# Attention value products on the quarters of the output partitions instead of the halves

## The chip, the cores and the metric

The kernel runs on one core of one Trainium2 chip. The metric is the device time of an execution in microseconds (us); lower is better. Three executions of the kernel before took 770.21, 770.67 and 775.93 us, so its time is given as the median, 770.67 us.

## What is computed

Four residual blocks follow one another on an image of 4 x 32 x 32 pixels with 32 channels, each on the channel-normalized input: a deformable convolution, a neighbourhood attention, a state-space block with three scan directions, and a convolution with learned offsets. Only the attention is touched. Cut to what matters:

```
qkv = x @ w_qkv + b_qkv                       # 32 channels -> q, k, v of 4 heads x 8
attn = einsum(q * scale, k of a 7 x 7 window) + relative bias
attn = softmax(attn over the 49 keys)
out  = einsum(attn, v of the same window)     # per head, 8 values a pixel
out  = out @ w_proj + b_proj
```

## The kernel before

Matrices lie with 128 partitions; `ps` is the accumulator memory, 8 banks of 512 float32 columns. The program is written per engine, and each engine runs its own list in order; semaphores named in `S("...")` connect them.

The attention works on one image (`b`) at a time. A *unit* is a pair of heads `m` (0 or 1) and two image rows of queries `i` (0 to 15): 64 queries (`QB`) for each of the two heads, which together fill 128 partitions, against 256 keys (`SPAN`), eight rows of the image in which the windows of these queries lie. That makes 32 units an image, in the order of `units` (all `i` of heads 0 and 1, then all `i` of heads 2 and 3). Four units are a *group* (`GROUP`), so there are 8 groups an image (`GPB`) and 32 in all (`NGROUP`).

For each group the engines do this:

- TensorE, `scores(g)`: 8 products, two units to a bank, one head each to partitions 0 to 63 or 64 to 127. In image 0 they are float32 with 128 rows (`k_own`), in the others bf16 with 72 rows.
- VectorE, `attend(g)`, lines 1257 to 1270: for each unit one pass over the 256 scores that adds the bias and takes the maximum (L1268, with a small copy before it or a copy of turned weights, below), `neg`.
- ScalarE, `attend(g)`: the exponential of each unit into `pexp` (L1619).
- TensorE, `turns(g)`: 8 transposes (L754), in two halves of four. The first half goes to bank 2 and waits for the exponentials of units 0 and 1, the second to bank 3 and waits for those of units 2 and 3. Each is released for the next group when its bank has been copied (`pt_v`, `pt_a`).
- The turned weights go to `pt`: bank 2 by VectorE in two copies (`copy_turned`, L1253, placed between the passes of units 2 and 3 of the next group), bank 3 by ScalarE in one (L1605, after the exponential of unit 1 of the next group).
- TensorE, `values(g)`: for each unit, for each of two blocks of 128 keys (`c`) and each head of the pair (`h`), one product of the values (128 keys x 64 columns, stationary) with 64 columns of turned weights. The 64 columns of `vz` are 32 channels of values, of which only the 8 of this head are not zero, and 32 columns of ones or zeros, which give the sum of the weights for the same head. Units 0 and 2 of a group go to partitions 0 to 63 of `ps`, units 1 and 3 to 64 to 127. Each float32 product is two matmul instructions in the trace, so a group has 32 of them for 16 products, and 16 or 8 for its scores.

The order on TensorE sets the software pipeline: in turn `g` of the loop come `scores(g)`, `turns(g - 1)`, `values(g - 2)`. In the trace `values(g - 2)` and `scores(g + 1)` thus stand side by side as one run of matmuls of L572, between two runs of transposes of L754.

The values of image `b` are placed in `vz` by VectorE (`place_values(b)`, four copies, L1245) ahead of group 2 of that image, after the last products of the image before. GpSimd has cleared `vz` and written the ones once, at the start (L1822, L1825). When an image is done, ScalarE copies its bank of sums to `ot_b` (L1611). At the end of the attention, TensorE turns them back in blocks (L806), VectorE divides by the sums of weights (a reciprocal at L1286 and a product at L1288, which the trace shows under the helper's line, L1055), TensorE turns the result (L813), and the projection follows.

Line 572 is the helper `mm`, line 1055 the helper `tt`, so groups of the trace under these lines are told apart by their shapes.

Of the kernel before, what the change touches and what calls it, by code (L numbers as in the profile page):

```python
# [116 lines left out]
def above(n):  # L117
    return n + LEAD
# [17 lines left out]
def build(nc, d, out):  # L136
    with ExitStack() as ctx:
# [116 lines left out]
        vt = cv(NV, P)  # L254
        vz = cv(NV, NH, 2, C)
        sc = cv(NSB, SPAN)
# [5 lines left out]
        ot_turned = cv(NBLK, B, C)  # L262
        rsum = cv(B, NBLK, NH)

# [303 lines left out]
        def _(pe):  # L568
# [190 lines left out]
            def values(g):  # L759

                b = g // GPB
                if g % GPB == 0:
                    pe.wait_ge(S("vz"), above(b + 1))
                    if b >= 2:
                        pe.wait_ge(S("ot_b"), above(b - 1))
                for q in (2 * g, 2 * g + 1):
                    pe.wait_ge(S("pt_a" if q % 2 else "pt_v"), above(q // 2 + 1))
                    for c in range(2):
                        for h in range(2):
                            for e in range(2):  # L770
                                m, i = units[(2 * q + e) % NUNIT]
                                at = QB * (i // 2)
                                v = V_ROWS.index(first_key_row(i) + 4 * c)
                                last = mm(ps[2 * C * e:2 * C * e + 2 * C, 4 + b % 2, at:at + QB],
                                          vz[:, v, 2 * m + h].rearrange("p a c -> p (a c)"),
                                          pt[:, (2 * q + e) % NRING, P * c + QB * h:P * c + QB * h + QB],
                                          start=(m == 0 and at == 0 and c == 0 and h == 0),
                                          stop=(m == 1 and c == 1 and h == 1), skip_group_check=True)
                last.then_inc(S("pv"), 1)
# [29 lines left out]
            for h in range(2):  # L809
                for i in range(4 * h, 4 * h + 4):  # L810
                    quad, odd = divmod(i % 4, 2)
                    to = ps[:, 4 + h, 2 * P * quad:2 * P * quad + 2 * P].rearrange("p (i r q) -> p i r q", i=2, r=2)[:, :, odd]
                    last = pe.transpose(to, ot_turned[:, i].rearrange("p b c -> p (b c)"), ident[:])  # L813
                last.then_inc(S("ot_back"), 1)
# [234 lines left out]
        def _(ve):  # L1049
# [189 lines left out]
            def place_values(b):  # L1239

                if b:
                    ve.wait_ge(S("pv"), above(b * GPB))
                ve.wait_ge(s_zero, 1)
                for n in range(NH):
                    last = ve.tensor_copy(vz[:, :, n, 0, HD * n:HD * n + HD], vt[:, :, bass.ds(b * C + HD * n, HD)])  # L1245
                last.then_inc(S("vz"), 1)
# [36 lines left out]
            for b in range(B):  # L1283
                ve.wait_ge(S("sums_turned"), b + 1)
                v = ps[:, b, :].rearrange("p (i a n d) -> p i a n d", i=NBLK, a=2, n=NH)
                own(ve.reciprocal(rsum[:, b], v[:, :, 1, :, 0]))  # L1286
                own.sync()
                tt(ot_turned[:, :, b].rearrange("p i (n d) -> p i n d", n=NH), v[:, :, 0],  # L1288
                   rsum[:, b].unsqueeze(3).to_broadcast([P, NBLK, NH, HD]), ALU.mult).then_inc(S("normalized"), 1)
            for h in range(2):  # L1290
# [483 lines left out]
        def _(gp):  # L1774
# [49 lines left out]
            for n in range(NH):  # L1824
                last = gp.memset(vz[:, :, n, 1, HD * n:HD * n + HD], 1.0)  # L1825
            last.then_inc(S("cleared"), 1)
# [188 lines left out]
```

## Time and profile before

| | us |
|---|---|
| median of three executions | 770.67 |
| the profiled execution | 771.34 |
| its span | 769.5 |
| TensorE busy, matmuls | 634.9 (82%) |
| VectorE busy | 662.3 (86%) |
| ScalarE busy | 503.2 (65%) |
| GpSimd busy | 454.2 (59%) |
| matmuls and other products under L572, share of the chain that ended last | 37% |
| transposes of L754, share of the same chain | 4% |

The span runs from the first to the last instruction; the time of an execution holds 1.8 us more. The attention lies between about 125 and 238 us of the span, its loop over groups between 134.6 and 229.6 us. The granted clock of TensorE is full (1.00) throughout the loop. The chain that ended last is followed backwards from the last instruction, each time to what released it; shares are of the whole span, of which the loop is an eighth.

### The profile page before, as it was taken

Reading aid. Unit: us, or ns where it says so; the run is one execution under the profiler, and the core shown is the slowest. Engines: PE = TensorE matmul, PEld = TensorE weight load, DVE = VectorE, ACT = ScalarE, POOL = GpSimd, SP = SyncE. Lnnn points to the kernel's source line nnn. Section 1 sums busy time; section 2 is a strip of 40 time slices with the busy share of each in tenths; the row PEclk is TensorE's granted clock in tenths of the full one; section 3 lists DMA queues with packets and bytes.
Section 4 is the critical chain, followed back from the end, with each engine's and each line's share of the span. In section 5 each row is a group of like instructions: output and inputs, shape, how many; then the busy total and the mean of one; then the engine's idle time right before and its main releaser. Section 6 shows DMA issues by size and latency. Waiting matters only on the chain.

```text
span 769.5 us, 11619 instructions
## 1 busy us (share of the span) xinstructions
PE 634.9 (82%) x3947; PEld 374.1 (49%) x3947; DVE 662.3 (86%) x902; ACT 503.2 (65%) x598; POOL 454.2 (59%) x282
## 2 busy tenths in 40 slices
PE   7899999999997961577676777777877879899997
PEld 5655547678884420244453444445544554233332
DVE  7899996779975979999999998999999865788886
ACT  2657613779974768587886876778777710477673
POOL 3798883000001066799999998898999740533321
PEclk9999999999999995599998886889898899899999
DMA  2004100440001031000000000000000004100000
GB/s 56 5 13 103 26 1 12 79 97 7 3 3 59 14 78 41 1 0 1 1 0 1 0 1 1 0 1 0 1 2 0 1 4 96 42 1 0 14 1 14
DMA packets 28854, 14.98 MB, mean 19 GB/s; under 512 B 23023, under 2 KB 24943, under 8 KB 28655
## 3 DMA queue, kind: packets, MB, share of 16 engines
q1 hardware_dynamic: 27582, 13.61, 8.3%
q10 hardware_dynamic: 1216, 0.66, 0.4%
q8 instruction: 32, 0.52, 0.3%
q14 instruction: 24, 0.19, 0.1%
HBM read 5.14 MB, written 0.78 MB: 8 GB/s over the span
## 4 chain that ended last, share of the span: by engine, by line
PE 41%; DVE 25%; issue 5%; ACT 5%; POOL 5%; DVEq 0%; POOLq 0%; ACTq 0%
PE ps L572 37%; DVE arena L1379 14%; DVE ps L1055 6%; PE ps L754 4%; POOL arena L1780 3%; DVE arena L1055 2%; ACT arena L1733 1%; POOL x3t L1780 1%; DVE arena L1330 1%; ACT x L1733 1%; DVE arena L1332 1%; ACT arena L1619 0%; DVE arena L1268 0%; ACT x1t L1733 0%; ACT arena L1720 0%
## 5 line engine op out<-in xcount | busy, mean ns | idle before, releaser
L572 PE MATMUL ps<-arena 128*64 128x64 f32 (+5 forms) x2072 | 357.6, 357 | 106.6 <-DVE arena L1379 34.7
L572 PEld LDWEIGHTS ps<-arena 128*64 128x64 f32 (+5 forms) x2072 | 140.7, 138 | 238.7 <-issue 95.0
L1780 POOL TENSOR_TENSOR arena<-arena 128x1024 f32<-128x1024 f32 x81 | 188.3, 2336 | 25.0 <-DVE arena L1379 8.5
L1379 DVE TENSOR_TENSOR_SCAN arena<-arena,ps 128x1024 f32<-128x1024 f32 x66 | 150.9, 2287 | 9.0 <-DVE ps L1055 0.5
L1765 ACT ACTIVATE arena<-ps,nycol 128x1024 f32<-128x1024 f32 x64 | 71.1, 1114 | 55.3 <-PE ps L572 55.3
L1055 DVE TENSOR_TENSOR ps<-arena,ps 128x1024 f32<-128x1024 f32 x75 | 91.0, 1213 | 6.3 <-PE ps L572 5.6
L1720 ACT ACTIVATE arena<-arena,a_col 128x1024 f32<-128x1024 f32 x66 | 75.4, 1142 | 16.9 <-DVE arena L1379 16.4
L1900 POOL TENSOR_TENSOR arena<-arena,bmask 128x128 f32<-128x128 f32 x64 | 30.8, 482 | 76.4 <-PE ps L572 65.3
L1379 DVE TENSOR_TENSOR_SCAN arena<-ps,arena 128x1024 f32<-128x1024 f32 x30 | 68.2, 2273 | 3.9 <-POOL arena L1780 2.4
L1055 DVE TENSOR_TENSOR arena<-ps,arena 128x512 f32<-128x512 f32 (+2 forms) x71 | 48.4, 683 | 24.9 <-PE ps L572 18.5
L1619 ACT ACTIVATE arena<-arena 128x256 f32<-128x256 f32 x128 | 60.8, 503 | 11.7 <-DVE arena L1268 7.6
L572 PE MATMUL ps<-ident,arena 128*128 128x128 f32 x416 | 64.7, 308 | 2.0 <-POOL arena L1780 2.0
L572 PEld LDWEIGHTS ps<-ident,arena 128*128 128x128 f32 x416 | 58.7, 162 | 15.0 <-issue 6.2
L1842 POOL MEMSET arena<- 128x6 f32 (+1 forms) x3 | 0.2, 102 | 105.6 <-DVE x2t L1293 105.6
L1733 ACT ACTIVATE arena<-ps 128x1024 f32<-128x1024 f32 x48 | 49.0, 1021 | 16.9 <-PE ps L572 16.1
L1268 DVE CUSTOM_DVE_ANT_0 arena<-ps,w_conv 128x256 f32<-128x256 f32 x124 | 51.1, 415 | 0.0
L1738 ACT ACTIVATE arena<-ps 128x1024 f32<-128x1024 f32 x30 | 30.8, 1025 | 25.6 <-PE ps L572 25.6
L1451 DVE TENSOR_SCALAR arena<-arena 128x1024 f32<-128x1024 f32 x64 | 47.0, 736 | 0.3 <-ACT arena L1765 0.3
L572 PE MATMUL ps<-arena,w_attn 96*128 96x512 bf16 (+1 forms) x132 | 41.1, 395 | 1.8 <-ACT arena L1765 0.9
L1101 DVE SCALAR_TENSOR_TENSOR arena<-ps,arena 128x1024 f32<-128x1024 f32 x32 | 37.1, 1219 | 3.3 <-ACT arena L1530 2.8
L754 PE MATMUL ps<-ident,arena 128*128 128x128 f32 x256 | 36.1, 281 | 1.9 <-ACT arena L1619 1.7
L1720 ACT ACTIVATE ps<-arena,a_col 128x1024 f32<-128x1024 f32 x30 | 33.4, 1114 | 3.8 <-DVE arena L1379 3.6
(208 smaller groups left out, 1049.9 us busy)
## 6 DMA issues: line engine op xcount, KB each, us to landing
arena<-arena SPq DMA_DIRECT2D x54, 64.0 KB
arena<-arena SPq DMA_DIRECT2D x12, 128.0 KB, 3.3
w_conv<-in_c_far SPq DMA_DIRECT2D x1, 1152.0 KB, 5.8
w_conv<-rpb_pad SPq DMA_DIRECT2D x36, 28.0 KB, 1.8
arena<-x SPq DMA_DIRECT2D x12, 64.0 KB, 2.0
arena<-x1t SPq DMA_DIRECT2D x12, 64.0 KB, 2.0
arena<-x3t SPq DMA_DIRECT2D x12, 64.0 KB, 2.0
arena<-arena SPq DMA_DIRECT2D x2, 288.8 KB, 3.7
```

Source lines behind the costliest of these rows:

```text
L572: return pe.matmul(o, l, r, start=start, stop=stop, **k)
L754: last = pe.transpose(ps[:, PT_BANKS[q % 2], side + P * c:side + P * c + P], pexp[:, (GROUP * g + e) % NRING, P * c:P * c + P], ident[:])
L1055: return ve.tensor_tensor(o, a, b, op)
L1101: return ve.scalar_tensor_tensor(out=square(o), in0=square(dx), scalar=0.0, in1=of, op0=sign, op1=ALU.mult)
L1268: ve.tensor_tensor_reduce(sc[:, n % NSB], ps[:, SC_BANKS[q % len(SC_BANKS)], SPAN * (e % 2):SPAN * (e % 2) + SPAN], bias(m, kind_of(i)), 1 ...
L1379: ve.tensor_tensor_scan(hs_ring[n % RING], decay, add, 0.0, ALU.mult, ALU.add).then_inc(S("scan"), 1)
L1451: ve.tensor_scalar(nhat[:, t % NU], ahat[:, t % NU], 1.0, 1.0, ALU.min, ALU.subtract).then_inc(S("nhat"), 1)
L1619: ac.activation(pexp[:, n % NRING], sc[:, n % NSB], ACT.Exp, bias=nmax[:, n % NSB:n % NSB + 1], scale=-1.0).then_inc(S("pexp"), 1)
L1720: ac.activation(bank2(2 * (n % 2)) if n in SHARED else da[:, n % 2], delta[:, t], ACT.Exp, scale=a_all[:, t * NS + n:t * NS + n + 1]).then ...
L1733: ac.activation(c_ring[n % RING], bank2(4), ACT.Copy).then_inc(S("c_copied"), 1)
L1765: ac.activation(ahat[:, t % NU].rearrange("p q n -> p (q n)"), bank2(2 * (t % 2)), ACT.Abs, bias=nycol[:, 0:1]).then_inc(S("abs"), 1)
L1780: return gp.tensor_tensor(o, a, b, ALU.mult)
```

## The change

- `vz` loses half its columns. An entry is now 32 columns wide: 8 columns for each of the two heads of a pair, of which one eight holds values and the other zeros, and 16 columns for the sums of weights in the same way.
- A value product now has 32 stationary columns and writes 32 partitions. The four units of a group go to the four quarters of the partitions, 0, 32, 64 and 96. The two pairs of heads, which shared columns and were told apart by zeros, now take the two halves of the bank's 512 columns.
- The number of products stays 16 a group, and each still streams 64 columns. The loop runs over all four units innermost, and both waits (`pt_v` and `pt_a`) stand ahead of the first product.
- The division reads the new layout. The reciprocal stays one instruction an image, the product is two, one for each pair of heads.
- The turning back at L813 writes its 8 blocks with other strides; their number is the same.
- GpSimd clears half as many elements of `vz`.

```diff
-        vz = cv(NV, NH, 2, C)
+        vz = cv(NV, NH, C)
...
-        rsum = cv(B, NBLK, NH)
+        rsum = cv(B, NH // 2, NBLK, 2)
...
-                for q in (2 * g, 2 * g + 1):
-                    pe.wait_ge(S("pt_a" if q % 2 else "pt_v"), above(q // 2 + 1))
-                    for c in range(2):
-                        for h in range(2):
-                            for e in range(2):
-                                m, i = units[(2 * q + e) % NUNIT]
-                                at = QB * (i // 2)
-                                v = V_ROWS.index(first_key_row(i) + 4 * c)
-                                last = mm(ps[2 * C * e:2 * C * e + 2 * C, 4 + b % 2, at:at + QB],
-                                          vz[:, v, 2 * m + h].rearrange("p a c -> p (a c)"),
-                                          pt[:, (2 * q + e) % NRING, P * c + QB * h:P * c + QB * h + QB],
-                                          start=(m == 0 and at == 0 and c == 0 and h == 0),
-                                          stop=(m == 1 and c == 1 and h == 1), skip_group_check=True)
+                pe.wait_ge(S("pt_v"), above(g + 1))
+                pe.wait_ge(S("pt_a"), above(g + 1))
+                for c in range(2):
+                    for h in range(2):
+                        for e in range(GROUP):
+                            m, i = units[(GROUP * g + e) % NUNIT]
+                            at = HALF // 2 * m + QB * (i // GROUP)
+                            v = V_ROWS.index(first_key_row(i) + 4 * c)
+                            last = mm(ps[C * e:C * e + C, 4 + b % 2, at:at + QB], vz[:, v, 2 * m + h],
+                                      pt[:, (GROUP * g + e) % NRING, P * c + QB * h:P * c + QB * h + QB],
+                                      start=(at == 0 and c == 0 and h == 0),
+                                      stop=(m == 1 and c == 1 and h == 1), skip_group_check=True)
                 last.then_inc(S("pv"), 1)
...
-                for i in range(4 * h, 4 * h + 4):
-                    quad, odd = divmod(i % 4, 2)
-                    to = ps[:, 4 + h, 2 * P * quad:2 * P * quad + 2 * P].rearrange("p (i r q) -> p i r q", i=2, r=2)[:, :, odd]
-                    last = pe.transpose(to, ot_turned[:, i].rearrange("p b c -> p (b c)"), ident[:])
+                for e in range(GROUP):
+                    to = ps[:, 4 + h, :].rearrange("p (i r q) -> p i r q", i=2, r=GROUP)[:, :, e]
+                    last = pe.transpose(to, ot_turned[:, GROUP * h + e].rearrange("p b c -> p (b c)"), ident[:])
...
-                    last = ve.tensor_copy(vz[:, :, n, 0, HD * n:HD * n + HD], vt[:, :, bass.ds(b * C + HD * n, HD)])
+                    h = n % 2
+                    last = ve.tensor_copy(vz[:, :, n, HD * h:HD * h + HD], vt[:, :, bass.ds(b * C + HD * n, HD)])
...
-                own(ve.reciprocal(rsum[:, b], v[:, :, 1, :, 0]))
+                own(ve.reciprocal(rsum[:, b], v[:, :, :, 1, :, 0]))
                 own.sync()
-                tt(ot_turned[:, :, b].rearrange("p i (n d) -> p i n d", n=NH), v[:, :, 0],
-                   rsum[:, b].unsqueeze(3).to_broadcast([P, NBLK, NH, HD]), ALU.mult).then_inc(S("normalized"), 1)
+                for m in range(NH // 2):
+                    last = tt(ot_turned[:, :, b, 2 * HD * m:2 * HD * m + 2 * HD].rearrange("p i (h d) -> p i h d", h=2), v[:, m, :, 0],
+                              rsum[:, b, m].unsqueeze(3).to_broadcast([P, NBLK, 2, HD]), ALU.mult)
+                last.then_inc(S("normalized"), 1)
```

On TensorE, in image 0, this is what stands between the transposes of one group and the scores of another, with the semaphores that each product waits for (`pt_v` and `pt_a` are the copies of turned weights by VectorE and ScalarE). Before:

```order
L754 MATMUL ps<-ident,arena 128x128 [waits pt_a,pexp]
L754 MATMUL ps<-ident,arena 128x128 x3
L572 MATMUL ps<-arena 64x64 [waits pt_v]
L572 MATMUL ps<-arena 64x64 x7
L572 MATMUL ps<-arena 64x64 [waits pt_a]
L572 MATMUL ps<-arena 64x64 x7
```

And now, at the same place:

```order
L754 MATMUL ps<-ident,arena 128x128 [waits pt_a,pexp]
L754 MATMUL ps<-ident,arena 128x128 x3
L572 MATMUL ps<-arena 32x64 [waits pt_a,pt_v]
L572 MATMUL ps<-arena 32x64 x15
```

The place in the program and the number of products are the same; the output of each is 32 partitions high instead of 64, and the wait for `pt_a` has moved from the ninth product to the first. The scores behind them keep their form of 64 partitions.

## Rows read from the trace of the kernel before

PE is TensorE, PEld its weight loads, DVE VectorE, ACT ScalarE. Starts are us from the start of the span.

**Rows 1.** windows: busy us (instructions) of PE, PEld, DVE, ACT, POOL; clock, DMA
```profile
145.00:163.00 18.00, 18.00 (x263) 13.24 (x258) 10.58 (x56) 11.41 (x25) 0.00 (x0) 1.00 0.53 92
194.00:222.00 28.00, 28.00 (x528) 23.73 (x528) 25.74 (x137) 25.43 (x57) 0.00 (x0) 1.00 0.01 3
```

**Rows 2.** the chain that ended last, value products and scores in turn with transposes
```profile
148.23 2.81 PE ps L572 x48
151.04 1.02 PE ps L754 x8
...
176.40 1.52 PE ps L572 x40
177.92 1.02 PE ps L754 x8
178.95 1.52 PE ps L572 x40
```

**Rows 3.** timeline, transposes and weight loads on PE: start, busy us, [idle before]
```profile
175.31 0.86 PEld L754 LDWEIGHTS ps<-ident,arena 128*128 128x128 f32 x8 [0.20 <-issue]
175.31 1.09 PE L754 MATMUL ps<-ident,arena 128*128 128x128 f32 x8
176.33 1.21 PEld L572 LDWEIGHTS ps<-arena 128*64 128x64 f32 x38 [0.17 <-issue]
```

**Rows 4.** timeline of the last groups on PE
```profile
225.13 1.15 PE L572 MATMUL ps<-arena 128*64 128x64 f32 x32
226.21 1.44 PE L754 MATMUL ps<-ident,arena 128*128 128x128 f32 x8
227.59 2.08 PE L572 MATMUL ps<-arena 128*64 128x64 f32 x64
229.60 0.93 PE L572 MATMUL ps<-w_dt,w_low 4*128 4x128 f32 x6
230.46 1.97 PE L806 MATMUL ps<-ident,arena 128*128 128x128 f32 x16
```

**Rows 5.** windows around four 32-column products of the last stage, columns as in rows 1
```profile
677.12:677.16 0.04, 0.04 (x5) 0.03 (x5) 0.04 (x1) 0.04 (x1) 0.00 (x0) 1.00 0.00 0
...
677.58:677.62 0.04, 0.04 (x8) 0.00 (x0) 0.04 (x1) 0.00 (x0) 0.04 (x1) 1.00 0.00 0
```

**Rows 6.** groups by line and form of the last stage, products to 32 partitions
```profile
L572 PE MATMUL ps<-arena 128*32 128x512 f32 x128 | 17.0, 605 | 0.8 <-DVE arena L1055 0.8
```

**Rows 7.** timeline of one group on VectorE and ScalarE
```profile
175.20 0.15 DVE L1267 COPY small<-ident 128x1 f32<-128x1 f32 x1 [0.25 <-PE ps L572]
175.27 0.41 DVE L1268 CUSTOM_DVE_ANT_0 arena<-ps,w_conv 128x256 f32<-128x256 f32 x1
...
176.17 0.42 DVE L1253 COPY arena<-ps 128x256 f32<-128x256 f32 x1
177.02 0.50 ACT L1619 ACTIVATE arena<-arena 128x256 f32<-128x256 f32 x1
177.64 1.14 ACT L1619 ACTIVATE arena<-arena 128x256 f32<-128x256 f32 x2
```

**Rows 8.** timeline, the last group: ScalarE releases the transposes and the values
```profile
225.82 1.13 ACT L1619 ACTIVATE arena<-arena 128x256 f32<-128x256 f32 x2
227.00 0.42 PEld L754 LDWEIGHTS ps<-ident,arena 128*128 128x128 f32 x4 [0.37 <-ACT arena L1619]
227.69 0.60 ACT L1605 ACTIVATE arena<-ps 128x512 f32<-128x512 f32 x1 [0.74 <-PE ps L754]
```

**Rows 9.** timeline: placing values, and the division after the attention
```profile
190.25 0.67 DVE L1245 COPY arena<-arena 128x144 f32<-128x144 f32 x4
231.55 0.42 DVE L1055 TENSOR_TENSOR arena<-ps,arena 128x256 f32<-128x256 f32 x1
231.89 0.35 DVE L1286 RECIPROCAL arena<-ps 128x32 f32<-128x32 f32 x1
```

More of the change, by code:

```diff
@@ L1284, in _ @@
                 ve.wait_ge(S("sums_turned"), b + 1)
-                v = ps[:, b, :].rearrange("p (i a n d) -> p i a n d", i=NBLK, a=2, n=NH)
-                own(ve.reciprocal(rsum[:, b], v[:, :, 1, :, 0]))
+                v = ps[:, b, :].rearrange("p (m i a h d) -> p m i a h d", m=NH // 2, i=NBLK, a=2, h=2)
+                own(ve.reciprocal(rsum[:, b], v[:, :, :, 1, :, 0]))
                 own.sync()
-                tt(ot_turned[:, :, b].rearrange("p i (n d) -> p i n d", n=NH), v[:, :, 0],
-                   rsum[:, b].unsqueeze(3).to_broadcast([P, NBLK, NH, HD]), ALU.mult).then_inc(S("normalized"), 1)
+                for m in range(NH // 2):
+                    last = tt(ot_turned[:, :, b, 2 * HD * m:2 * HD * m + 2 * HD].rearrange("p i (h d) -> p i h d", h=2), v[:, m, :, 0],
+                              rsum[:, b, m].unsqueeze(3).to_broadcast([P, NBLK, 2, HD]), ALU.mult)
+                last.then_inc(S("normalized"), 1)
             for h in range(2):
@@ L1824, in _ @@
             for n in range(NH):
-                last = gp.memset(vz[:, :, n, 1, HD * n:HD * n + HD], 1.0)
+                h = n % 2
+                last = gp.memset(vz[:, :, n, 2 * HD + HD * h:2 * HD + HD * h + HD], 1.0)
             last.then_inc(S("cleared"), 1)
```

## The prediction

> **What bounds the kernel now.** I read three views in this order: the windows, for the busy time of each engine in the attention; the chain that ended last, for what the end waits for there; the timeline of one group, for the slack of the rest. In the loop over groups TensorE is busy all the time at a granted clock of 1.00, in image 0 and later [rows 1]. In the chain of waits the loop is almost nothing but TensorE: five runs of 48 matmuls at 2.81 us (values and float32 scores of image 0), 24 runs of 40 or 36 (values and bf16 scores), nearly all at 1.52 us, each followed by eight transposes at 1.02 us [rows 2]. So a turn of the loop takes 3.83 us in image 0 and 2.54 later, and what the value products give back is on the path. But the others are close: from 194 to 222 us VectorE is busy 25.74 of 28 us and ScalarE 25.43; up to 163 us they have room (10.58 and 11.41 of 18) [rows 1]. The question is how much of TensorE's gain a turn can use before another engine holds it.
>
> **What a value phase costs now.** The last groups show it without scores behind. One group's 32 matmuls and the change to transposes take 226.21 - 225.13 = 1.08 us; two groups' 64 take 229.60 - 227.59 = 2.01 [rows 4]. The second 32 thus cost 0.94, which is 29 ns each, or 0.059 a round of two (one per half of the partitions), and 0.14 is left for starting a phase of another form. Transposes agree: sixteen are busy for 1.97 us and eight for 1.09, so eight more cost 0.11 each [rows 3, 4], and the 1.02 of a turn is 8 x 0.11 + 0.14. A turn after image 0 is then 0.88 + 0.14 for the transposes, 0.94 + 0.14 for the values, and what is left of the 1.52, 0.44, for the scores. At each of the two changes of form in a turn the weight loads stand idle for 0.17 to 0.20 us, released by nothing but issue; between values and scores, both 64 columns wide, they run on without a gap (one row of loads, x38) [rows 3].
>
> **What four quarters cost.** The number of matmuls stays 32; the question is whether four run at once. The last stage has products of 128 rows to 32 partitions, float32, 512 columns, in turn on the four quarters. Four are under way within 0.04 us of the first (x5, with one that was running before), and by 0.5 us later the next four start [rows 5]; 128 of them took 17.0 us, 0.133 each, while one alone lasts 0.605 [rows 6]. So quarters do run together, at float32 and with different streams. A round of four is taken at the price of a round of two now, 0.059, since both stream 64 columns: 8 rounds, 0.47 us instead of 0.94. Against it stands a third change of form in each turn, from 32 columns back to the scores' 64. No row has this change; the two that rows have, between 128 and 64, cost 0.14 each, nothing is the other bound, and I take 0.14, the nearest row. Net gain for a value phase: 0.94 - 0.47 - 0.14 = **0.33 us**.
>
> The Trainium skill, TensorEngine Tiling (Array Packing), Key Properties, speaks against the change here: a change of tiling mode drains the array, a change of tile does not. The idle weight loads at each change in rows 3 agree with it for 128 and 64 columns; by it the sum has the third change, without it the turn would gain 0.47.
>
> **What the turn can use.** There is a chain through three engines over two turns. From the start of the transposes at 175.31 [rows 3]: VectorE copies the first bank at 176.17, +0.86, then passes unit 2, copies again and passes unit 3, and ScalarE starts the last exponential at 177.64, +1.47; it takes 0.50 [rows 7] and another 0.05 to release TensorE (225.82 + 1.13 to 227.00, [rows 8]). That is 2.88 us from the first transpose to the second half of the next group's transposes. Where these are released late, the values follow after 0.59 (227.00 to 227.59, [rows 4, 8]), and values and scores take the 1.52. Together 4.99 us for two turns, 2.50 each, against 2.54 on TensorE: the two are nearly tied now. With 0.33 less it is 4.66, or **2.33** a turn, while TensorE alone would need 2.21. VectorE's own work is a third bound: four passes and two copies of 256 elements, each of which lets the next start after 0.34 (231.55 to 231.89, [rows 9]), and two small copies at 0.07 (175.20 to 175.27, [rows 7]): 2.18. So the turn goes from 2.54 to 2.33, and 0.12 of the 0.33 becomes a wait of the transposes for ScalarE's exponential (L1619), perhaps twice that in every second turn.
>
> **The sum**, for the profiled execution of 771.3 us:
> - Image 0: 5 phases, VectorE has room, the full gain: 5 x 0.33 = 1.65.
> - The other 24: 24 x 0.21 = 5.0.
> - VectorE places the values of images 1 to 3 within a turn, 0.67 us each [rows 9]. Its slack a turn falls from 2.54 - 2.18 = 0.36 to 0.15, so each costs about 0.2 more: -0.6.
> - The last two value phases. The last must now wait at its start for ScalarE's copy, 227.69 + 0.60 + 0.05 = 228.34 [rows 8]; with 0.47 + 0.14 it ends at 228.95, where TensorE went on at 229.60 [rows 4]: 0.65.
> - The division: one product of 256 elements, after which VectorE starts anew 0.34 us later [rows 9], becomes two of 128, for each of four images, all on the path. No row has the half. Copies of 144 elements take 0.17 each [rows 9], so that nothing is lost, and two at the old price lose 0.34 each; nearest is the 0.07 of a copy of one element, as the constant of one more instruction [rows 7]: -0.3.
> - GpSimd's smaller clearing ends long before the first use and counts nothing, as the loads of q and k do, which are not waited for; the earlier wait for `pt_a` counts nothing within the loop: ScalarE's copy of a group (0.60, [rows 8]) comes after one exponential of the next, while the values that need it stand behind a run of scores and one of transposes. If that cover were gone, each turn would lose up to those 0.60. The turning back has the same eight transposes.
>
> 1.65 + 5.0 - 0.6 + 0.65 - 0.3 = 6.4 us. 771.3 - 6.4 = 764.9; this execution lay 0.7 above the median of the three, so 764.2.
>
> **The rivals.**
> - *No third change of form* (columns 32 to 64 without the 0.14): 0.47 a phase. The chain gives (4.99 - 0.47)/2 = 2.26, so 24 x 0.28 + 5 x 0.47 + 0.65 + 0.14 for the end, less 0.8 for the placing and 0.3: 8.8, **761.8**. For it: no row shows a cost for 32 against 64. Against: both other changes cost.
> - *TensorE sets the pace* at 2.21, the chain over three engines being shorter than I add it: 24 x 0.33 + 1.65 + 0.65 - 1.0 - 0.3 = 8.9, **761.7**. Against: in the last group the second half of the transposes does wait for ScalarE, 0.37 [rows 8].
> - *Slower: the matmuls cannot follow each other closer than 29 ns.* In the value phases no row has them closer over any length; the quarters of rows 5 come in a burst of four and then wait 0.4 us. If issue is what holds the rate, 32 still cost 0.94 and the third change of form is added: a turn of 2.68, 29 x 0.14 + 0.3 = 4.4 us lost, **775.0**. It decides from 0.8 us for the 32, 25 ns each, where the gain is used up: **770.9** with the division. Against: within 0.04 us four matmuls with their weight loads started.
> - The Trainium skill, TensorE: Matmul & The Clock Gate (Wait — 56ns, not 53.3ns?), has such a floor: starts never closer than about 25 ns however few columns. By it the 32 would cost 0.80, the case just named; rows 5 disagree for a burst on different quarters.
>
> **How the numbers follow.** Forecast 0.55, no third change 0.13, TensorE's pace 0.10, issue-bound 0.14 (half of it at no gain, half slower), 0.08 for shifts in the later stages by some us. A measurement tells about 1% from no change. Faster by over 1% means below 763.0: the two better cases for the most part and a fifth of the forecast, 0.30. Slower by over 1% (above 778.4) needs the bad case and more: 0.04. The forecast's own range is 762.5 to 766.5. The range takes in both better cases and goes most of the way to no gain: 760.8 to 769.5; left out are the issue-bound cases and part of the shifts.
>
> **What would show it.** Turns of 3.50 us up to 162 us and of about 2.33 after; 1.52 down to about 1.2 for a run of values and bf16 scores; a third idle time of the weight loads ("issue") in each turn, ahead of the scores; PEld of L754 waiting for ACT L1619, about 3 us in all over the loop; VectorE nearly without idle time; division steps longer by 0.07. Wrong if the runs of values keep 29 ns a matmul, if turns stand at 2.2 or 2.5, or if the loop is shorter by 6 us and the whole isn't.

## The result, and the profile after

The changed kernel takes **766.32 us** (median of 13 runs, 763.08 to 768.73); the kernel before took 770.84 in the 13 runs beside them (767.59 to 775.93). The ratio is 0.9928, with a 95% interval of 0.9906 to 0.9951: faster by 3.8 to 7.2 us, by less than 1%, which the prediction took as the least that a measurement tells from no change. The forecast was 764.2, in a range of 760.8 to 769.5. The two profiled executions took 771.34 and 767.62 us.

The span of the changed kernel's profile is 765.8 us, only 3.7 less than before (769.5). Where the two differ must be read stage by stage, so I go to the loop first. The chain that ended last, within the loop:

```profile
144.13 2.46 PE ps L572 x48
...
147.61 2.46 PE ps L572 x48
...
194.04 0.85 ACT arena L1620 x2
195.36 0.51 ACT arena L1620
195.87 0.43 DVE arena L1267 x2
...
197.14 0.44 ACT arena L1606
197.62 0.50 ACT arena L1620
...
198.66 0.85 ACT arena L1620 x2
```

In image 0 it is TensorE alone as before [rows 2], but a run of 48 takes 2.46 us instead of 2.81, and a turn 147.61 - 144.13 = 3.48 instead of 3.83. After image 0 the chain has left TensorE: it goes through ScalarE's exponentials (L1620), its copy (L1606) and VectorE's passes (L1267), and repeats after 198.66 - 194.04 = 4.62 us. That is two turns, 2.31 each; before, a turn was 2.54.

The timeline of two such turns, on TensorE and its weight loads (start, busy us, what ended the idle time before):

```profile
171.29 1.21 PE L572 MATMUL ps<-arena 128*32 128x64 f32 x40
...
172.43 0.86 PEld L754 LDWEIGHTS ps<-ident,arena 128*128 128x128 f32 x8 [0.20 <-ACT arena L1620]
...
173.46 1.21 PE L572 MATMUL ps<-arena 128*32 128x64 f32 x40
...
174.60 1.39 PE L754 MATMUL ps<-ident,arena 128*128 128x128 f32 x8
...
175.33 0.42 PEld L754 LDWEIGHTS ps<-ident,arena 128*128 128x128 f32 x4 [0.31 <-ACT arena L1620]
...
175.92 0.88 PE L572 MATMUL ps<-arena 128*32 128x64 f32 x34
```

One turn's values start 2.17 us before the next one's (171.29 to 173.46), and those 2.46 before the next (to 175.92). The turns alternate so, but for those in which VectorE places the values of the next image (2.73 to 2.80 us). In the long one the eight transposes come in two fours, and the second four wait for ScalarE's exponential.

The waits of the loop, summed (engine, tile and line that wait, releaser: us, times, longest). After:

```profile
PEld ps L754 <- ACT arena L1620: 7.5, 27, 0.4
PEld ps L572 <- issue: 5.5, 32, 0.3
```

And before, in the loop as it lay then:

```profile
PEld ps L572 <- issue: 5.2, 31, 0.2
...
PEld ps L754 <- ACT arena L1619: 0.9, 3, 0.4
```

The wait of the transposes for ScalarE grew from 0.9 to 7.5 us, more than the turns lost by it, as will be seen. The idle times of the weight loads of L572 by issue hardly changed in number: one a turn.

What the value products cost, with the groups by form. After, from 160 to 215 us (count | busy us, mean ns of one | idle):

```profile
L572 PE MATMUL ps<-arena 128*32 128x64 f32 x736 | 15.0, 222 | 0.0
```

Before, from 163 to 222 us, the same number:

```profile
L572 PE MATMUL ps<-arena 128*64 128x64 f32 x736 | 26.5, 225 | 0.0
```

736 are 23 groups of 32. One group's run was 26.5 / 23 = 1.15 us long and is 0.65 now. A single matmul lasts as long as ever (225 and 222 ns), so from the first start to the last it was 0.93 and is **0.43 us**, 14 ns for each of the 31 steps where it was 30. In the starts four follow each other within 20 ns, one per quarter, and the next four begin 56 ns after them; before it was a pair every 58 ns.

The last groups on TensorE, which answer to [rows 4]:

```profile
218.25 0.65 PE L572 MATMUL ps<-arena 128*32 128x64 f32 x32
...
220.42 0.65 PE L572 MATMUL ps<-arena 128*32 128x64 f32 x32
221.27 0.65 PE L572 MATMUL ps<-arena 128*32 128x64 f32 x32 [0.19 <-ACT arena L1606]
221.85 0.93 PE L572 MATMUL ps<-w_dt,w_low 4*128 4x128 f32 x6
...
226.70 1.09 PE L811 MATMUL ps<-ident,arena 128*128 128x128 f32 x8 [2.02 <-DVE arena L1053]
228.13 3.48 PE L572 MATMUL ps<-arena,w_attn 128*128 128x512 f32 x4 [0.34 <-ACT arena L1634]
```

The last values wait for ScalarE's copy (L1606). The loop ends at 221.85 us instead of 229.60, 7.75 earlier. The stage of the scans behind the attention begins at 301.44 instead of 309.11, 7.67 earlier. From there to the end 4.0 us are given back; a section of its own, below, is about these.

### The profile page after: what moved, and what is told of

It reads as the page before. It is cut to its first block, busy times and chain, and to the rows that moved or that the text cites. A ratio compares the mean times of both kernels' runs of the same rounds, so it can differ in the third digit from the quotient of the medians.

```text
span 765.8 us, 11653 instructions
## 1 busy us (share of the span) xinstructions
PE 626.2 (82%) x3947; PEld 359.6 (47%) x3947; DVE 660.8 (86%) x906; ACT 502.1 (66%) x598; POOL 453.1 (59%) x282
## 4 chain that ended last, share of the span: by engine, by line
PE 40%; DVE 37%; ACT 9%; issue 8%; POOL 4%; DVEq 0%; DMA 0%; SPq 0%; ACTq 0%; POOLq 0%
PE ps L572 38%; DVE arena L1380 14%; DVE ps L1053 8%; DVE arena L1053 4%; DVE arena L1099 4%; ACT arena L1620 3%; POOL arena L1781 3%; DVE ps L1099 2%; PE ps L754 1%; ACT arena L1734 1%; DVE arena L1267 1%; ACT x L1734 1%; DVE arena L1331 1%; PE ps L633 1%; ACT arena L1606 1%
## 5 line engine op out<-in xcount | busy, mean ns | idle before, releaser
L572 PE MATMUL ps<-arena 128*32 128x64 f32 (+5 forms) x2072 | 345.5, 357 | 110.7 <-DVE arena L1380 37.1
L572 PEld LDWEIGHTS ps<-arena 128*32 128x32 f32 (+4 forms) x2072 | 125.3, 124 | 245.9 <-issue 97.4
L572 PE MATMUL ps<-ident,arena 128*128 128x128 f32 x416 | 65.9, 312 | 2.0 <-POOL arena L1781 2.0
L572 PEld LDWEIGHTS ps<-ident,arena 128*128 128x128 f32 x416 | 59.3, 164 | 14.5 <-issue 5.4
L1620 ACT ACTIVATE arena<-arena 128x256 f32<-128x256 f32 x128 | 59.0, 502 | 6.2 <-DVE arena L1267 4.7
L1267 DVE CUSTOM_DVE_ANT_0 arena<-ps,w_conv 128x256 f32<-128x256 f32 x124 | 50.9, 414 | 0.0
L572 PE MATMUL ps<-arena,w_attn 96*128 96x512 bf16 (+1 forms) x132 | 42.3, 406 | 1.8 <-ACT arena L1766 0.9
L754 PE MATMUL ps<-ident,arena 128*128 128x128 f32 x256 | 38.4, 283 | 3.7 <-ACT arena L1620 2.3
L1721 ACT ACTIVATE ps<-arena,a_col 128x1024 f32<-128x1024 f32 x30 | 33.4, 1115 | 4.3 <-DVE arena L1380 4.0
```

The source lines that it names most:

```text
L572: return pe.matmul(o, l, r, start=start, stop=stop, **k)
L754: last = pe.transpose(ps[:, PT_BANKS[q % 2], side + P * c:side + P * c + P], pexp[:, (GROUP * g + e) % NRING, P * c:P * c + P], ident[:])
L1267: ve.tensor_tensor_reduce(sc[:, n % NSB], ps[:, SC_BANKS[q % len(SC_BANKS)], SPAN * (e % 2):SPAN * (e % 2) + SPAN], bias(m, kind_of(i)), 1 ...
L1620: ac.activation(pexp[:, n % NRING], sc[:, n % NSB], ACT.Exp, bias=nmax[:, n % NSB:n % NSB + 1], scale=-1.0).then_inc(S("pexp"), 1)
L1721: ac.activation(bank2(2 * (n % 2)) if n in SHARED else da[:, n % 2], delta[:, t], ACT.Exp, scale=a_all[:, t * NS + n:t * NS + n + 1]).then ...
```

## The experiments

Three things were open. Why do four quarters take 14 ns a matmul and not 30: is it the width of the weights, the streams side by side, or the order? Is the third change of form real? And what holds the turn after image 0?

**1. The order of the four units.** If quarters run side by side only where neighbours in the program stand on different quarters, two pairs in turn must fall back to two at a time, and one unit after the other to one.

```diff
-                for c in range(2):
-                    for h in range(2):
-                        for e in range(GROUP):
+                for e0, c, h, r in [(e0, c, h, r) for e0 in (0, 2) for c in range(2) for h in range(2) for r in range(2)]:
+                    e = e0 + r
...
```

> As the changed kernel (32 columns, quarters), but only two quarters take turns at a time: units 0 and 1, then 2 and 3. If the gain comes from four matmuls at once and each turn has one change of form more (0.10 us in the changed kernel's trace), the values cost 16 rounds of 0.059 again, a turn after image 0 lasts 2.64 us, the loop over groups 98 us (95.0 before, 87.4 changed), and the kernel is slower than before by about 3 us. If narrower outputs alone were what helps, loop and time stay near the changed kernel's.

```diff
-                for c in range(2):
-                    for h in range(2):
-                        for e in range(GROUP):
+                for e in range(GROUP):
+                    for c in range(2):
+                        for h in range(2):
```

> As the changed kernel, but each unit's four products follow one another on one quarter. If a quarter is held by its own stream of 64 columns, the 32 matmuls cost 0.058 us each, 1.9 us, a turn 3.5 us after image 0, and the loop some 25 us more than before, about 120 us. If matmuls of one quarter followed at the rate of issue, the loop would stay under 90 us.

Both lost less than that. The chain of the kernel in pairs, then that of the serial one:

```profile
195.44 1.39 PE ps L572 x40
...
197.90 1.39 PE ps L572 x40
...
200.32 1.39 PE ps L572 x40
```

```profile
196.74 1.88 PE ps L572 x40
...
199.65 1.88 PE ps L572 x40
```

The turns are 2.46 and 2.42 us in turn in pairs (2.64 expected) and 2.91 serial (3.5 expected). The chain is TensorE alone in both. The times: 768.32 (10 runs) against 771.60, ratio 0.9967 (0.9933 to 1.0), hardly told from no change, but not the loss that was expected; and 780.48 in one run. One group's 32 matmuls take 0.68 us from first to last start in pairs, where 0.93 was expected, and 1.18 serial. The starts suggest why. In pairs two matmuls start at a time, about 56 ns apart, up to 0.25 us; there four start within 20 ns. Only 8 have started by then, and 8 more of units 0 and 1 stand ahead of units 2 and 3 in the program. The trace doesn't name the unit of a matmul, but the best reading is that one whose quarter is free passes those that wait for another quarter. If so, one quarter for all must give back the whole price, whatever the order.

**2. One quarter for all.** The sums of the four units then mix on the same 32 partitions, so the output isn't the attention's; the kernel is there for its time alone.

```diff
-                            last = mm(ps[C * e:C * e + C, 4 + b % 2, at:at + QB], vz[:, v, 2 * m + h],
+                            last = mm(ps[0:C, 4 + b % 2, at:at + QB], vz[:, v, 2 * m + h],
```

> As the changed kernel, but the products of all four units go to partitions 0 to 31 and add up there, so the output is not the reference's. Theory A: a quarter is held for 56 ns by each matmul of 64 float32 columns, whatever weights are ready, and matmuls of other quarters are started ahead of it; then the 32 matmuls take 31 x 0.056 = 1.74 us from first to last start (0.435 on four quarters, 0.68 in pairs, 1.18 with the units one after another). Theory B: matmuls start in program order, and a quarter can take the next after 25 to 30 ns; then the 32 take as long as with the units one after another or less, 1.2 us at most.

One group's run at the end of the loop, in the timeline:

```profile
252.38 1.97 PE L572 MATMUL ps<-arena 128*32 128x64 f32 x32
```

1.97 less the 0.22 of the last is 1.75 us for 31 steps, 56 ns each; the turn is 3.48 us and the time 802.47 (one run). So a quarter takes a matmul of 64 float32 columns every 56 ns. Over four quarters that gives 14 ns, which is what the changed kernel has. In program order the serial kernel would need 56 ns for nearly every step, as here; it takes 1.18 us instead of 1.75, so the next unit's quarter must begin before the last one's is done. That matmuls are taken out of order fits all three, and an order kept strictly fits neither the serial kernel nor the one in pairs; how it is decided which may pass, these runs don't tell.

**3. Weights or streams.** I had said that a round would keep its price, 0.059, "since both stream 64 columns". Half of the streamed columns, in either kernel, tests that; half of the queries then get no output.

```diff
-                                last = mm(ps[2 * C * e:2 * C * e + 2 * C, 4 + b % 2, at:at + QB],
+                                last = mm(ps[2 * C * e:2 * C * e + 2 * C, 4 + b % 2, at:at + C],
...
-                                          pt[:, (2 * q + e) % NRING, P * c + QB * h:P * c + QB * h + QB],
+                                          pt[:, (2 * q + e) % NRING, P * c + QB * h:P * c + QB * h + C],
```

> The kernel before with 32 of the 64 columns of turned weights streamed in each value product, so half of the queries get no output. Is the 58 ns of a round of two the stream's or that of the weights (64 columns each)? If the stream of 64 columns sets it, a round falls to 30 ns and the 32 matmuls from 0.93 to about 0.48 us; if loading 2 x 64 columns of weights sets it, they stay at 0.93.

The same edit of the two slices in the changed kernel:

> The changed kernel with 32 of the 64 columns streamed in each value product, so half of the queries get no output. If the stream sets the 56 ns of a round of four, it falls to about 29 ns and the 32 matmuls from 0.435 to about 0.25 us; if loading 4 x 32 columns of weights sets it, they stay at 0.435. A matmul would then start each 7 ns, which is the closest spacing in any row; if issue is slower than that over a length, something between comes out.

The kernel before with half the stream, then the changed one (groups by form):

```profile
L572 PE MATMUL ps<-arena 128*64 128x32 f32 x676 | 23.9, 224 | 0.0
```

```profile
L572 PE MATMUL ps<-arena 128*32 128x32 f32 x768 | 11.0, 199 | 0.0
```

With 64 weight columns half the stream brings next to nothing: a group's run is 1.13 us instead of 1.15, a turn 2.52 instead of 2.54. With 32 it brings nearly half: 24 groups in 11.0 us, 0.46 each instead of 0.65. From first to last start that is 0.26 us, 8 ns a matmul, 32 ns a round of four. In image 0 the turn falls from 3.48 to 3.29. So before, it wasn't the stream that set the round of 58 ns, for the round stayed when the stream was halved. What is left is the loading of 64 columns of weights; nothing here separates it from what else goes with outputs of 64 partitions. Now the stream sets the round (56 ns), and loads of 32 columns take 32 ns or less a round, side by side on the four quarters. The times were 775.25 and 763.18, one run each, too few to say more.

**4. The third change of form.** Scores in products of 32 queries have the values' form, so the change goes; the number of float32 products doubles.

```diff
-                    for h in range(2):
-                        o = ps[QB * h:QB * h + QB, SC_BANKS[q % len(SC_BANKS)], side:side + SPAN]
+                    for h, r in ((0, 0), (0, 1), (1, 0), (1, 1)):
+                        o = ps[QB * h + C * r:QB * h + C * r + C, SC_BANKS[q % len(SC_BANKS)], side:side + SPAN]
+                        queries = slice(QB * i + C * r, QB * i + C * r + C)
```

> As the changed kernel, but the scores are also written in quarters: 16 products of 32 queries a group instead of 8 of 64, so that values and scores have one form. If the change from 32 to 64 columns costs 0.10 us, image 0 loses 0.10 a turn (3.48 to 3.38), the later turns 0.05 (the chain over three engines takes half): the loop goes from 87.4 to about 85.7 us. If the change costs nothing, or if the twice as many score products cost more than they save, the loop stays at 87.4 or grows.

The chain in image 0:

```profile
145.34 2.31 PE ps L572 x64
...
148.68 2.31 PE ps L572 x64
```

Values and scores take 2.31 us where the changed kernel has 2.46, and 16 more instructions cost nothing that shows. Between the last value matmul's start and the first score's there were 0.052 us in the kernel before, 0.149 in the changed one, and 0.036 here. That is 0.10 more than before, and not all: in image 0 the second pair of score matmuls starts 0.27 us after the first pair in the changed kernel and 0.22 in the kernel before, 0.05 more. The change of form is thus real, 0.15 us in image 0 in all, and taking it away gives back the same 0.15; after image 0 it is about 0.12. The kernel takes **762.77** (4 runs), ratio 0.9874 (0.9805 to 0.9943). Its loop ends at 221.2 us, 0.65 earlier than the changed kernel's, though its first turn in the chain starts 1.2 us later (145.34, and 144.13 there).

**5. What holds the turn.** VectorE copies the turned weights between its passes, so that the last pass, and the exponential behind it, are late. Here the copies stand behind the four passes, and each pair of passes has one small copy ahead of it, so that VectorE's work in a turn stays what it was.

```diff
-                    ve.wait_ge(S("sc"), above(q + 1))
+                    if e % 2 == 0:
+                        ve.wait_ge(S("sc"), above(q + 1))
...
-                    if e >= 2 and g:
-                        copy_turned(g - 1, e - 2)
-                    else:
+                    if e % 2 == 0:
...
+                if g:
+                    for e in range(2):
+                        copy_turned(g - 1, e)
```

> As the changed kernel, but VectorE copies the turned bank after its four passes instead of between them, and does one of the two small copies of a pair less, so that its own work stays at 2.18 us a turn. If the chain VectorE copy, pass, exponential, transposes holds the turn at 2.31, it now falls to 2.18 to 2.22 and the loop from 87.4 to about 84.5 us, the waits of the transposes for the exponential go from 7.5 to under 2 us. If the work of VectorE or ScalarE itself or TensorE sets 2.31, the loop stays at 87 us.

The waits of the loop:

```profile
PEld ps L754 <- ACT arena L1622: 8.8, 26, 0.8
```

The turns are 2.165 and 2.27 us instead of 2.165 and 2.46, and the loop ends at 219.75, 2.1 earlier. The time is 763.88 (4 runs), ratio 0.9895 (0.9809 to 0.9981). The gain came, the reason was half wrong: under 2 us of waiting for ScalarE were expected, and 8.8 are there. So VectorE's order held every second turn, and something else the other, at 2.165. Both edits together show what:

> The changed kernel with scores in quarters and VectorE's copies behind its passes, both at once. The change of form is gone for TensorE and the chain over three engines is broken, so VectorE's own 2.18 us sets the turn: 24 turns at 2.18 to 2.22 and image 0 at 3.33 instead of 3.48. The loop falls from 87.4 to about 83.8 us and the kernel to about 3.5 us under the changed one. If another chain holds the turn, it stays at the 2.25 of the better of the two alone, a loop of 84.8 us or more.

A window of its later images (busy us of PE, PEld, DVE, ACT, POOL, each with its instructions; clock; DMA), then the timeline of VectorE and ScalarE over a turn and the placing behind it, and two waits of TensorE:

```profile
192.00:214.00 22.00, 20.68 (x561) 16.49 (x560) 22.00 (x125) 21.95 (x52) 0.00 (x0) 1.00 0.02 4
```

```profile
198.03 0.14 DVE L1266 COPY small<-ident 128x1 f32<-128x1 f32 x1
198.09 0.41 DVE L1267 CUSTOM_DVE_ANT_0 arena<-ps,w_conv 128x256 f32<-128x256 f32 x1
...
198.43 0.42 DVE L1267 CUSTOM_DVE_ANT_0 arena<-ps,w_conv 128x256 f32<-128x256 f32 x1
...
198.78 0.14 DVE L1266 COPY small<-ident 128x1 f32<-128x1 f32 x1
198.84 0.41 DVE L1267 CUSTOM_DVE_ANT_0 arena<-ps,w_conv 128x256 f32<-128x256 f32 x1
...
199.18 0.42 DVE L1267 CUSTOM_DVE_ANT_0 arena<-ps,w_conv 128x256 f32<-128x256 f32 x1
...
199.53 0.75 DVE L1253 COPY arena<-ps 128x256 f32<-128x256 f32 x2
199.85 1.76 ACT L1623 ACTIVATE arena<-arena 128x256 f32<-128x256 f32 x4
200.20 0.14 DVE L1266 COPY small<-ident 128x1 f32<-128x1 f32 x1
...
202.36 0.65 DVE L1245 COPY arena<-arena 128x144 f32<-128x144 f32 x4
...
202.82 0.58 ACT L1615 ACTIVATE arena<-ps 128x512 f32<-128x512 f32 x1
...
202.93 0.14 DVE L1266 COPY small<-ident 128x1 f32<-128x1 f32 x1
```

```profile
196.07 0.86 PEld L755 LDWEIGHTS ps<-ident,arena 128*128 128x128 f32 x8 [0.33 <-ACT arena L1623]
...
198.23 0.86 PEld L755 LDWEIGHTS ps<-ident,arena 128*128 128x128 f32 x8 [0.33 <-ACT arena L1623]
```

A turn is now 2.16 us but where values are placed (196.07 to 198.23), the transposes wait for ScalarE in each, and VectorE and ScalarE are busy for 22.00 and 21.95 of 22. Which of the two has no room? The placing of values doesn't tell. It adds 202.93 - 202.36 = 0.57 us to VectorE and lengthens its turn by as much, from 200.20 - 198.03 = 2.17 to 202.93 - 200.20 = 2.73, but in the same turn ScalarE copies the finished image's sums (L1615, 0.58), so both have more to do. VectorE's starts tell. From 198.03 they follow each other after 0.06, 0.34, 0.35, 0.06, 0.34 and 0.35 us, and the two copies take the 0.67 up to 200.20: no step of 256 elements is more than 0.01 longer than where nothing was waited for (0.34, [rows 9]). VectorE thus doesn't wait in this turn, and **VectorE's own work is the floor**: two small copies, four passes and two copies of 256 elements make the 2.16. ScalarE is nearly as full. Its exponentials start every 0.40 to 0.46 us and its copy takes up 0.49; with all four at 0.40 a turn would be 2.09, an estimate from these steps, so it has 0.07 to spare. As its exponential is the last link to TensorE, the wait bears its name. Image 0 has its turns at 3.33 as expected. This kernel takes **759.82 us** (6 runs, 758.22 to 764.77) against 772.76, ratio 0.9845 (0.9812 to 0.9878), the fastest here.

**6. The same two kernels again**, for what differs between executions.

> The changed kernel once more. In its profile the loop over groups is 7.75 us shorter, the start of the scans 7.7 us earlier, but the whole 3.7 us shorter: from the first scan on it took 4.0 us more, with the clock of TensorE halved for 82 us of the scans instead of 75. If this is the chance of one execution, this profile keeps the 7.7 us at the first scan and has another figure from there on, and the median lies 5 to 8 us under before; if the change causes it, the stretch from the first scan on is again 464 us against 460.

> The kernel before once more, for a second profile of the stretch from the first scan to the end. In the profiles so far this took 460.4 to 461.3 us in five kernels, with the clock halved for 99 to 105 us of it, and 463.5 to 464.6 in five others, with 112 to 115 us. If the change caused the longer one, the kernel before shows 460 again each time; if it is drawn by each execution, 464 can come here too. The loop is 95.0 us and the first scan starts at about 309.

> The changed kernel a third time, beside the kernel before on the same chip, for the difference of the medians and a third profile. If each execution draws its share of halved clock, the profile may show 460 from the first scan on, and over all runs the difference comes near the 7.7 us of the loop. If it shows 464 a third time, the change or where it puts the scans makes the long stretch likelier, and the difference stays at 5 to 6 us.

The changed kernel gave 765.68 (6 runs, ratio 0.9913, 0.9883 to 0.9942) and 764.13 (6 runs, ratio 0.989, 0.9862 to 0.9918); the kernel before 771.59 (12 runs) beside another 17 of its own at 772.76. All 25 runs of the changed kernel together have a mean of 765.6 us, the 66 of the kernel before that ran beside it or the experiments 772.0: **6.4 us**, and by the spread of these runs between 5.4 and 7.3.

## The four microseconds after the attention

The windows from the first scan to the end, columns as above, for the kernel before (profiled twice):

```profile
309.10:769.50 460.40, 364.46 (x1713) 201.02 (x1712) 400.07 (x325) 307.90 (x299) 329.18 (x200) 0.89 0.04 8
```

```profile
310.10:774.60 464.50, 370.20 (x1713) 204.96 (x1712) 400.95 (x325) 308.23 (x299) 329.38 (x200) 0.87 0.04 8
```

And for the changed kernel (the first of its three profiles, and the third):

```profile
301.40:765.80 464.40, 365.67 (x1713) 201.78 (x1712) 400.50 (x326) 308.24 (x299) 329.36 (x200) 0.88 0.04 8
```

```profile
301.20:762.20 461.00, 365.00 (x1713) 201.03 (x1712) 399.97 (x325) 308.13 (x299) 329.18 (x200) 0.88 0.04 8
```

The instructions are the same and VectorE's busy time agrees to 1 us. The length is 460.4 or 464.5 us for the kernel before and 464.4 or 461.0 for the changed one (464.4 in the second profile), so that either kernel has both. Over all 13 profiles it lies between 460.3 and 464.6, while TensorE's clock was granted at half, 1.2 GHz, for 99 to 120 us of it. They fall in two groups: seven with 99 to 110 us at half are 460.3 to 461.3 long, six with 112 to 120 are 463.5 to 464.6. The two profiles that I first compared had drawn the short tail for the kernel before and the long one for the changed one: 4.0 of the 7.7 us that the profile seems to lose are no effect of the change that these profiles can show. The prediction had named as a sign of being wrong that the loop is shorter by 6 us and the whole isn't; the first two profiles, 3.7 us apart, show just that, and only the repeated runs answer it. Whether the change makes the long tail likelier (two of three profiles, against one of two) so few profiles can't tell. What makes an execution draw the one or the other stays open.

The clock shows within the attention's end too. The window from the loop's end to the next projection, after and before:

```profile
221.80:235.50 13.70, 9.47 (x63) 6.83 (x53) 7.23 (x20) 3.93 (x7) 3.04 (x8) 0.88 0.15 42
```

```profile
229.60:241.50 11.90, 7.92 (x57) 6.18 (x53) 6.97 (x16) 3.93 (x7) 3.04 (x8) 1.00 0.18 48
```

In the changed kernel the clock is at half (0.50 in a window of its own) from 227.8 to 231.2 us, behind the wait of 2.02 us for the division, and the projection of the attention (L572, w_attn) takes 3.48 us; before it took 1.98 at full clock. In the kernel before the stretch at half came later, from 241.6 to 245.0 us, in the run of matmuls behind, which took 33.4 us there and 31.7 here. So 1.5 us are lost at one place and 1.7 won at the next.

## Why the prediction was right, step by step

**Two at a time against four.** The 32 matmuls were put at 0.47 us instead of 0.94 and took 0.43 instead of 0.93; the change between values and scores was put at 0.14 and cost 0.15 in image 0. The net gain of a phase was put at 0.33 and is 0.35 there (2.81 to 2.46). The five turns of image 0 gave 1.74 us (1.65 forecast). The reason given was only half right: it is not that the stream alone set the old round and stayed. The old round of 58 ns didn't follow the stream; it took the narrower weights and outputs to leave the stream as the bound, at 56 (experiment 3). That the two are so close, and a round of four could be priced like a round of two, was luck.

**A floor for a matmul's start.** The rival at 29 ns (775.0) and the one at 25 ns (770.9) are out: 32 matmuls start within 0.43 us, 14 ns a step, and 8 ns with half the stream. The Trainium skill, TensorE: Matmul & The Clock Gate, Wait — 56ns, not 53.3ns?, from which the second came, doesn't hold here across quarters. On a single quarter no step was under 55 ns (experiment 2), so that nothing there bears on it.

**The third change of form.** No such cost would have meant 761.8; it is there, at 0.12 to 0.15 us. By the Trainium skill, TensorEngine Tiling (Array Packing), Key Properties, a change of tiling mode drains the array; that the gap goes from 0.149 to 0.036 us when scores get the values' form agrees. The sign that I named for it was wrong: no third idle time of the weight loads by issue appears ahead of the scores (32 in all for L572, 31 before). It shows only in the starts.

**The turn after image 0.** 2.33 forecast, 2.31 measured; two turns 4.66 and 4.62. Every second turn is held by the chain over three engines: standing the copies behind the passes takes 0.19 from each (2.46 to 2.27). The other turns, at 2.17, are TensorE's own need, 1.14 from the first value product to the first transpose (171.29 to 172.43) and 1.03 for the transposes: the rival of TensorE's pace (2.21 a turn, 761.7) thus holds in every second turn and not in all. VectorE's own work was put at 2.18, and experiment 5 finds it at 2.16, just as long, so that TensorE's faster pace alone would bring nothing more in these turns either. The changed kernel with half the stream shows both at once: its values take 0.17 us less, its short turns stay at 2.16 and its long ones fall to 2.27. Two turns together thus give up what one value phase gives up (4.62 to 4.43, with 0.02 less between values and scores), and in pairs they grow by what one grows (0.25, to 4.87). That fits the chain as it was forecast, two turns long and with the values in it once. The chain that the profile follows in the loop (above) names other links, ScalarE's copy and no values, and alone would not have shown this.

**The wait of the transposes.** About 3 us in all were forecast, and the sum shows 7.5. But where a turn is short, the wait reads 0.20 by ScalarE and the transposes take their 1.03; the same 0.20 stood there before with the name issue [rows 3]: it is the change of form under another name. In the long turns the transposes take 1.32 (174.60 to 175.92) instead of 1.03, 0.29 lost in each of ten, 2.9 us; the three turns with a placing lose 0.57 to 0.63 each. This is the wait that I meant, "perhaps twice" 0.12 in every second turn; the number that I named as its sign was the wrong one to name.

**Placing, ends, division.** From the end of image 0 to the last two value phases 5.16 us were won, 4.4 forecast (5.0 less 0.6). The 24 turns of the forecast gave 4.86 of it. At 0.23 each they would give 5.6, so that the placing cost 0.7 where 0.6 was put. The other 0.29 come from one more turn, that of the last group with values alone (225.13 to 227.59 before, 218.25 to 220.42 now), which the sum left out. The last two value phases gave 0.58 (0.65 forecast), with the predicted wait for ScalarE's copy (0.19). The division cost 0.26 (0.3 forecast). In its timeline, which answers to [rows 9], two products of 128 elements and the next reciprocal:

```profile
223.80 0.49 DVE L1053 TENSOR_TENSOR arena<-ps,arena 128x128 f32<-128x128 f32 x2
224.20 0.35 DVE L1285 RECIPROCAL arena<-ps 128x32 f32<-128x32 f32 x1
```

It is 0.40 us from the first product to the next reciprocal, where it was 0.34: the 0.07 of one more instruction was the right bound, the 0.34 of another full product the wrong one.

**The sum.** In the loop and its ends 1.74 + 5.16 + 0.58 - 0.26 = 7.2 us, and the loop started another 0.27 earlier in this execution; 6.4 was forecast. Of the missing 0.8, 0.3 is the turn that was left out and 0.5 the later turns at 0.23 instead of 0.21; the small misses of the other terms cancel. The means of all runs differ by 6.4 us too, but that this is the forecast to the tenth is luck, since the terms sum to 7.2 and the difference is known to about 0.9.

The forecast of 764.2 lay 2.1 us below the first median. Little of that is its base, the median of three runs: 770.67, where 13 runs gave 770.84. The rest is that the medians of these 13 and 13 runs differ by only 4.5 us. Their means differ by 5.6 and those of all runs by 6.4, for single runs of either kernel spread over 6 to 10 us, and a median of few moves with the long or short tail that they draw.

## What to carry to other kernels

Count every engine's own work in a turn beside the chains between engines: where they are nearly tied, a faster engine gives back only down to the next floor (here 0.23 of 0.35 us), and the engine that the wait names need not be the one that holds it. In these runs products whose outputs stand on different quarters of the partitions ran side by side at the pace of the stream, once weights and outputs were 32 wide. Products of the same form should stand together, as the change of form cost 0.12 to 0.15 us here. And when two profiles differ by 4 us in a stage that the change did not touch, profile the same kernels again before explaining it.

## What the hardware showed that I had not expected

- Matmuls seem to start ahead of others that stand before them in the program, where these wait for another quarter; it is read from the starts, as no record names its unit. One quarter: 56 ns a matmul, 1.75 us for 32; one unit after another: 1.18 us for 32 instead of 1.75; in pairs: 0.68 instead of 0.93.
- With 32 streamed columns on four quarters a matmul with its own weight load started every 8 ns (0.26 us from the first of 32 to the last), though each lasts 199 ns.
- Sixteen more matmuls in a turn of image 0 cost nothing that shows where they saved a change of form (2.46 to 2.31 us).
- The stage from the first scan to the end, about 460 us, ran at half clock for 99 to 120 us of it in the 13 profiles, and its length moved by up to 4 us, in the kernel before alone from 460.4 to 464.5. A change of 6 us in 770 needs many runs of both kernels.
